# A rebuilt start of the program in a fused attention and expert kernel: loads in order of need, statistics a batch at a time, splits on VectorE, keys loaded before queries

## The chip, the core and the metric

The kernel runs on one core of a Trainium2 chip. The core has a matrix engine (TensorE, PE in the profile; its weight loads are PEld), VectorE (DVE), ScalarE (ACT), GpSimd (POOL) and SyncE (SP), which here only issues DMAs. The metric is the time of one execution on the device in microseconds, the median of several. Each engine works through its own list in program order; a semaphore makes an instruction, and all behind it on that engine, wait for another engine or a DMA.

## The reference

For 4 batches of 1,024 rows of 128 floats the reference computes

```
mod = silu(c) @ wmod -> sa, ca, ga, sb, cb, gb per batch   (ga, gb kept at least 0.25 in size)
h   = layernorm(x) * (1 + ca) + sa
Q, K, V = h @ W.T + b, 16 heads of 8
scores  = Q K^T / sqrt(8) + lambda * (tanh(Q) J) tanh(K)^T, causal, softmax
x   = x + ga * (attended @ Wo.T + bo)
h   = layernorm(x) * (1 + cb) + sb
expert = argmax(h @ centroids.T), one of 8;  y = layernorm(h) through that expert's two layers of 512
x   = x + gb * (alpha * y + (1 - alpha) * h)
```

## The kernel before, in words

Names: `X` holds all rows. `T32` holds Q, K, tanh(K), tanh(Q)J (and tanh(Q)) of one batch as 128 channels by 1,024 rows; `T16` holds each of the four as a sum of three bf16 parts. A score is a bf16 product over 96 rows of parts; the parts go to DRAM (`q_parts`, `k_parts`) and come back into `stacks`, one region for each of the four groups of four heads, query side and key side apart (`load_group`: 3 loads for queries, 6 for keys, one for values `Vs`). A softmax without overflow needs each query's maximum first: for every group a list of 22 "maxima" chunks (`CHUNKS`, kind m) is multiplied on PE and reduced on VectorE (L1443, L1450), the result is split in three bf16 parts (`mparts`, L1462 to L1464), turned on PE (kind T), copied to `mrow` and sent by four DMAs (L376) into `stacks` as 3 more rows, against three rows of ones on the key side (99 rows in all). Then PE makes scores (L1014), ScalarE the exponentials (L785), PE the products with the values (L989).

The program has a start ("prologue"), then 4 bodies of 4 groups ("first", two "middle" in a loop, "last"), then the experts' tiles. In a body, the maxima of the group after are woven into the attention of the present one, by a planner (`schedule`): it is given a cost for each item (`D_COST`, `P_COST`, `R_COST`) and spreads the items so that VectorE's costs grow in step with PE's. Items: P (projections of the next batch, in group 0), D (VectorE alone) and R (after attention). `schedule(prep, post, last)` puts the items of `POST_AT` or `POST_LAST` in the groups.

The prologue, which is what changes. SP loads the first batch of X, wmod, the four weights, the other batches, and then `JB`, a 128x128 block diagonal matrix, by 16 small loads into a zeroed tile (L359). ScalarE issues 7 loads of `rows` (vectors that PE turns into columns, `cols`), 4 of biases (`bias_in`, the last of them `b2_b`, 512 KB), and, after its first activation, the expert weights W1 and W2 and beta. VectorE: `base` (L1146), `cols` (L1149), silu of the conditioning (L1153 on), weights out of PSUM (L1158), statistics of batch 0 (L1164, then 15 steps of a Newton root, `moment_step`, each waiting for the one before), `JL` (L1172), `modT`, normed rows (L1140), and the evacuation of the ten P items in the order X, Q, K, V, J. After the small product for `modT` (L862) PE makes the wide one (L865) that gives the other modulations, `MB`, before the projections. GpSimd splits the first of the four tensors (L574 to L579), VectorE the other three (`split0`, three steps each: subtract, cast, subtract), then come `conditioning` (which turns the wide product into `MB`) and the statistics of the three other batches (L1164 again, 24 at once). SP stores each tensor's parts when it is split, waits for GpSimd to say that all are stored, and loads groups 0 and 1 (L366, L369). PE turns the expert weights (`turn_weights`, 16 in all, evacuated by ScalarE, L762 and L764): four before the maxima of group 0, one after each of the first twelve chunks. GpSimd writes the rows of ones (L563), two regions at the start, two after `fold_beta` (L590 to L598: beta through W1, and b1), and adds `ga_bo` to X (`residual`, L611).

## Time and profile before

| | us |
|---|---|
| median of 3 runs | 845.47 (844.82 to 854.59) |
| the profiled execution, its own time | 847.08 |
| its span, first to last instruction | 845.2 |
| first projection on PE | 27.09 |
| first chunk of maxima on PE | 67.38 |
| first score of the first attention group | 106.38 |

| engine | busy us | share |
|---|---|---|
| PE | 694.1 | 82% |
| DVE | 620.3 | 73% |
| ACT | 455.9 | 54% |
| POOL | 250.6 | 30% |

A timeline row gives start, length, engine, line and operation, what is written and read, and in brackets the idle time before it with what ended it. A shared name covers several tiles (arenaA, arenaB), and a helper's line (L1111 is every `tensor_tensor`) covers many operations, so one goes by time and shape.

### The profile page before, as it was taken

To read this page: it belongs to the slowest core of one execution; us is meant where nothing else is said; L and a number is where in the kernel's file an instruction comes from. 1 tells how busy PE (TensorE), PEld (TensorE's weight loads), DVE (VectorE), ACT (ScalarE), POOL (GpSimd) and SP (SyncE) were. 2 spreads that over 40 slices of the span, in tenths; PEclk is the share of its full clock that TensorE was granted. 3 is DMA by queue.
4 is the path that set the end of the run, shared out by engine and by line. 5 is a ranking of instruction groups with operands and counts; after the bars stand their busy time and mean duration, and the time that the engine had idled before them with its cause. 6 is when DMAs were issued, how large, how long until landed. Compare 5 with 4: busy or idle time off the path is not lost.

```text
span 845.2 us, 17049 instructions
## 1 busy us (share of the span) xinstructions
PE 694.1 (82%) x5087; PEld 348.3 (41%) x5087; DVE 620.3 (73%) x1485; ACT 455.9 (54%) x1077; POOL 250.6 (30%) x210
## 2 busy tenths in 40 slices
PE   3517597999999899888798987999988879886694
PEld 1314143333343334233333333433423326876694
DVE  6698977778778887878487878778887812786453
ACT  0213065667665575546456754557564668644482
POOL 5205803930000860114028502030001400453643
PEclk9758589999999999989799999999999979997898
DMA  9389190419533237525403392436302243621520
GB/s 260 132 209 255 43 177 1 124 55 168 113 69 61 77 104 145 97 53 134 102 14 92 90 183 57 86 109 144 123 16 90 113 147 105 194 65 66 191 77 12
DMA packets 51305, 91.96 MB, mean 109 GB/s; under 512 B 9005, under 2 KB 24945, under 8 KB 50700
## 3 DMA queue, kind: packets, MB, share of 16 engines
q1 hardware_dynamic: 41904, 67.56, 34.2%
q0 software_dynamic: 6400, 17.86, 6.8%
q10 hardware_dynamic: 2908, 5.41, 2.0%
q8 instruction: 46, 0.75, 0.4%
q14 instruction: 47, 0.39, 0.2%
HBM read 51.05 MB, written 37.90 MB: 105 GB/s over the span
## 4 chain that ended last, share of the span: by engine, by line
PE 51%; DVE 22%; issue 11%; DMA 6%; SPq 5%; ACT 2%; DVEq 1%; POOL 0%; ACTq 0%; POOLq 0%
PE PS L989 13%; PE PS L1014 12%; PE PS L952 10%; DVE PS L1443 5%; PE PS L1065 4%; PE PS L1076 3%; DVE arenaB L1111 3%; SPq L376 3%; DVE block_max L1450 2%; PE PS L1018 2%; DMA arenaA<-mrow 2%; ACT arenaA L785 2%; PE PS L892 2%; DMA arenaB<-r_den 1%; DVE arenaA L1111 1%
## 5 line engine op out<-in xcount | busy, mean ns | idle before, releaser
L785 ACT ACTIVATE arenaA<-PS 128x512 f32<-128x512 f32 (+3 forms) x768 | 332.0, 494 | 251.4 <-PE PS L1018 190.4
L1443 DVE CUSTOM_DVE_ANT_0 PS<-PS,mask 128x1024 f32<-128x1024 f32 (+3 forms) x256 | 261.3, 1037 | 71.9 <-PE PS L952 63.9
L1014 PE MATMUL PS<-arenaA 99*128 99x512 bf16 (+3 forms) x768 | 225.4, 340 | 17.3 <-DMA arenaA<-mrow 7.9
L952 PE MATMUL PS<-arenaA 96*128 96x512 bf16 (+3 forms) x768 | 202.7, 341 | 36.3 <-DVE maxima L1443 19.8
L989 PE MATMUL PS<-arenaA,Vs 128*9 128x512 f32 (+3 forms) x1536 | 164.2, 504 | 0.0
L1014 PEld LDWEIGHTS PS<-arenaA 99*128 99x128 bf16 x768 | 73.8, 99 | 207.3 <-ACT arenaA L785 122.5
L1450 DVE TENSOR_REDUCE block_max<-PS 128x8 f32<-128x1024 f32 (+1 forms) x96 | 100.3, 1045 | 24.3 <-PE PS L957 23.1
L952 PEld LDWEIGHTS PS<-arenaA 96*128 96x128 bf16 x768 | 66.5, 101 | 107.3 <-DVE maxima L1443 46.5
L1018 PE MATMUL PS<-after,identb 128*128 128x128 bf16 x512 | 107.6, 227 | 0.0
L574 POOL TENSOR_TENSOR arenaB<-arenaB 128x1024 f32<-128x1024 f32 x13 | 27.9, 2144 | 197.6 <-ACT arenaB L724 197.5
L677 POOL DMA_INDIRECT out_dram<-arenaA x46 | 46.1, 1001 | 98.2 <-DVE arenaA L1111 94.8
L831 ACT ACTIVATE arenaA<-PS,b1p 128x128 f32<-128x128 f32 x184 | 52.9, 372 | 38.0 <-PE PS L1065 37.8
L1065 PE MATMUL PS<-arenaA 128*128 128x128 f32 x368 | 53.3, 292 | 15.0 <-DVE arenaA L1532 14.9
L630 POOL TENSOR_TENSOR arenaB<-arenaB,MB 128x1024 f32<-128x1024 f32 x4 | 9.5, 2366 | 159.7 <-DVE arenaB L1111 159.7
L1065 PEld LDWEIGHTS PS<-arenaA 128*128 128x128 f32 x368 | 47.9, 204 | 18.2 <-DVE arenaA L1532 18.2
L1018 PEld LDWEIGHTS PS<-after,identb 128*128 128x128 bf16 x512 | 52.0, 101 | 4.0 <-issue 0.2
L1076 PE MATMUL PS<-arenaA 128*128 x368 | 51.7, 287 | 1.8 <-issue 1.8
L957 PE MATMUL PS<-identb,after 128*128 128x128 bf16 x256 | 51.5, 230 | 0.0
L1076 PEld LDWEIGHTS PS<-arenaA 128*128 128x128 f32 x368 | 47.8, 203 | 2.4 <-issue 2.4
L989 PEld LDWEIGHTS PS<-arenaA,Vs 128*9 128x9 f32 x1536 | 23.7, 89 | 51.2 <-ACT arenaA L785 24.8
L654 POOL DMA_INDIRECT by_expert<-arenaB,slot x32 | 31.2, 977 | 29.3 <-issue 14.3
L1532 DVE COPY arenaA<-PS 128x128 f32<-128x128 f32 x46 | 13.0, 285 | 32.7 <-PE PS L1056 32.0
(179 smaller groups left out, 726.7 us busy)
## 6 DMA issues: line engine op xcount, KB each, us to landing
arenaA<-k_parts SPq DMA_DIRECT2D x96, 128.0 KB, 7.3
arenaA<-by_expert SPq DMA_DIRECT2D x46, 192.5 KB, 3.4
o_raw<-OT SPq DMA_DIRECT2D x32, 256.0 KB, 2.2
arenaA<-q_parts SPq DMA_DIRECT2D x16, 384.0 KB, 5.1
q_parts<-arenaB POOLq DMA_DIRECT2D x18, 256.0 KB, 3.8
k_parts<-arenaB POOLq DMA_DIRECT2D x18, 256.0 KB, 3.8
arenaA<-q_parts SPq DMA_DIRECT2D x16, 256.0 KB, 5.7
w_turned<-arenaA SPq DMA_DIRECT2D x2, 2048.0 KB, 9.4
```

The lines of the kernel that those rows point to most:

```text
L677: g.indirect_dma_start(out_rows, bass.IndirectOffsetOnAxis(ap=XSI[n % NX][:, 3 * D:3 * D + 1], axis=0), YS[:, n % U, :], None, bounds_chec ...
L785: a.activation(PT[:, u % EB, h, off:HALF], PS[:, 4 + n % SB_, off:HALF], ACT.Exp).then_inc(exp_ok, 1)
L831: last = a.activation(HR[:, n % 3, k * P:(k + 1) * P], PS[:, 3 + n % 2, k * P:(k + 1) * P], ACT.Relu, bias=b1p[:, bass.ds(expert[n] * FC + ...
L952: last = mm(PS[:, place + c0 // HALF, at:at + c1 - c0], SQ(g, h)[0:KROWS, t * P:(t + 1) * P], SK(g, h)[0:KROWS, c0:c1], start=(at == 0), s ...
L957: last = mm(diag, after[:, :], identb[:, :], start=False, stop=True, skip_group_check=True)
L989: last = mm(PS[32 * h:32 * h + VW, 7, off:HALF], Vs[:, g, (kb * HG + h) * VW:(kb * HG + h + 1) * VW], PT[:, u % EB, h, off:HALF], start=(k ...
L1014: last = mm(bank[:, off:HALF], SK(g, h)[0:MROWS, kb * P:(kb + 1) * P], SQ(g, h)[0:MROWS, qc * HALF + off:(qc + 1) * HALF], start=True, sto ...
L1018: last = mm(bank[:, off:off + P], identb[:, :], after[:, :], start=False, stop=True, skip_group_check=True)
L1065: last = mm(PS[:, 3 + n % 2, k * P:(k + 1) * P], W1C[n % 3][:, k * P:(k + 1) * P], XT[:, n % 3, :], start=(k == 0), stop=True, skip_group_ ...
L1076: last = mm(PS[:, 6 + n % 2, 0:D], HR[:, n % 3, k * P:(k + 1) * P], W2T[:, bass.ds(expert[n] * FF + k * P, P)], start=(k == 0), stop=(k == ...
L1443: v.tensor_tensor_reduce(out=src, in0=src, in1=mask[:, S - n:S], scale=1.0, scalar=-3e38, op0=ALU.add, op1=ALU.max, accum_out=maxima[:, pl ...
L1450: v.tensor_reduce(block_max[:, place % 2, heads[0]:heads[-1] + 1, t, 0:t + 1], src.rearrange("p h (c q) -> p h c q", q=P), AX.X, ALU.max). ...
```

## The change

1. SP loads the weights ahead of wmod, `J` in one load (`Jr`, 128x8) behind them, then the other batches; rows of ones come by DMA from `onesb` (two regions early, two just before groups 2 and 3 are loaded), and W1 and W2 now come on SP's queue. W1 is read so that each partition gets 4 adjacent rows (2 KB runs). ScalarE issues 5 loads of rows, the same 4 of biases, then `b1c` (b1 in runs of 4 floats) and beta, all ahead of its first activation.
2. VectorE begins with the statistics of batch 0; `JL` is made from `Jr` and a mask `of_head`; the weights' evacuation is ScalarE's; only the small product for `modT` stands ahead of the projections, the wide one behind them.
3. P items in the order X, Q, K, J, V. Statistics of batch 1 lie between them, those of batches 2 and 3 in groups 1 and 2 of the first body.
4. All four splits of batch 0 on VectorE, with ScalarE casting the middle part of two. Key parts are waited for and loaded apart from and ahead of query parts for group 0.
5. Six weights are turned ahead of the maxima; `fold_beta` works in pieces of a quarter or a half; no ones on GpSimd.

What moves on VectorE at the start of the program. Before (`silu` is the conditioning, `lnt` the root of the statistics, `arenaB<-silu` the wide copy of silu for the wide product):

```order
L1146 TENSOR_SCALAR base<-iota_f 128x8 [waits consts_ok]
L1149 COPY cols<-PS 128x62 [waits cols_ps]
L1151 TENSOR_SCALAR bqs<-cols 128x1 [waits cols_ok]
L1153 TENSOR_SCALAR silu<-silu 128x4 [waits silu_e]
L1154 RECIPROCAL silu<-silu 128x4 [waits dve_chain]
L1111 TENSOR_TENSOR silu<-silu,cols 128x4 [waits dve_chain]
L1156 COPY arenaB<-silu 128x512 [waits dve_chain]
L1158 COPY wT<-PS 128x512 [waits wT_ps]
L1164 BN_STATS stat<-X 128x6 [waits x_in0]
```

The same place now, from the first statistics on (L1137 is the helper's line now):

```order
L1174 BN_STATS stat<-X 128x6 [waits x_in0]
...
L1185 COPY cols<-PS 128x22 [waits cols_ps,dve_chain]
...
L1189 TENSOR_SCALAR bqs<-cols 128x1 [waits cols_ok,dve_chain]
L1191 TENSOR_SCALAR silu<-silu 128x4 [waits silu_e]
L1192 RECIPROCAL silu<-silu 128x4 [waits dve_chain]
L1137 TENSOR_TENSOR silu<-silu,cols 128x4 [waits dve_chain]
L1166 TENSOR_SCALAR arenaB<-X,lnt 128x128 x8
L1495 COPY arenaA<-silu 128x512 [waits silu3_ok]
L1499 SCALAR_TENSOR_TENSOR JL<-Jr,lam_c,of_head 128x128 [waits bias_in,consts_ok,j_in]
L1502 COPY modT<-PS 128x4 [waits mod_ps]
L1503 TENSOR_SCALAR modT<-PS 128x4
L1233 TENSOR_SCALAR HT<-PS,modT 128x512 [waits max_ps,modT_ok]
```

Statistics and root (not all rows shown) went ahead of the conditioning, `base` and `wT` left this stretch, and JL waits for the bias loads with the normed rows already made.

VectorE's splits now, after the second K evacuation (L1241 are the two J evacuations, the last L1137 a V evacuation):

```order
L1239 TENSOR_SCALAR arenaB<-PS,cols 128x512 [waits max_ps,dve_chain]
L1137 TENSOR_TENSOR arenaB<-arenaB 128x1024 [waits max_used,first_ok]
L1516 CAST arenaB<-arenaB 128x1024 [waits r1_ok]
L1137 TENSOR_TENSOR arenaB<-arenaB 128x1024 [waits split0_step,r1_ok]
L1137 TENSOR_TENSOR arenaB<-arenaB 128x1024 [waits first_ok]
L1241 COPY arenaB<-PS 128x512 [waits max_ps] x2
L1516 CAST arenaB<-arenaB 128x1024 [waits max_used,r1_ok]
L1137 TENSOR_TENSOR arenaB<-arenaB 128x1024 [waits split0_step,r1_ok]
L1137 TENSOR_TENSOR arenaB<-arenaB 128x1024 [waits first_ok] x2
L1137 TENSOR_TENSOR arenaB<-arenaB 128x1024 [waits mid_ok,r1_ok] x2
L1137 TENSOR_TENSOR arenaB<-PS,bv_b 128x16x8 [waits max_ps]
```

Before, V and J were evacuated first, then three splits of subtract, cast, subtract followed.

SP between the last stored parts and the loads of group 0, now:

```order
L412 DMA q_parts<-arenaB 16x8x1024 [waits split0_ok]
L412 DMA q_parts<-arenaB 16x8x1024 x2
L376 DMA arenaA<-k_parts 16x4x1024 [waits parts0_k]
L376 DMA arenaA<-k_parts 16x4x1024 x5
L376 DMA arenaA<-q_parts 48x4x1024 [waits parts0_q]
L376 DMA arenaA<-q_parts 32x4x1024
L386 DMA Vs<-arenaB 128x288 [waits va_ok]
```

Before, the 3 query loads came first and all ten waited for all twelve stores.

The diff, cut to what the text speaks of:

```
@@ tiles
+        Jr = sb("Jr", [P, HD])
+        of_head = sb("of_head", [P, H])
+        b1c = sb("b1c", [P, E, FC])
@@ planner
-        FIRST = [("P", 0, k) for k in range(len(PREP))] + [("m", 0, k) for k in range(NM)] + \
+        FIRST = [("P", 0, PREP.index(step)) for step in ("X0", "X1", "Q0", "Q1", "K0", "K1", "J0", "J1", "V0", "V1")] + [("m", 0, k) for k in range(NM)] + \
+        STATS_AT = {g: ((4, "D", ("stats_b", b_)),) + tuple((5 + n // 2, "D", ("root_b", b_, n)) for n in range(MOMENTS)) for g, b_ in ((1, 2), (2, 3))}
+        D_COST = {("stats_b", b_): 1600 for b_ in (2, 3)} | dict(denominators=870, ...
-        BODIES = dict(first=schedule(True, False, False), middle=schedule(True, True, False), last=schedule(False, True, True))
+        BODIES = dict(first=schedule(True, STATS_AT, False), middle=schedule(True, POST_AT, False), last=schedule(False, POST_LAST, True))
@@ SyncE
-            sp.dma_start(wm[:, :], wmod).then_inc(w_in, 16)
             for n, w in enumerate((Wq, Wk, Wv, Wo)):
                 sp.dma_start(wraw[:, n, :], w).then_inc(w_in, 16)
+            sp.dma_start(wm[:, :], wmod).then_inc(w_in, 16)
+            sp.dma_start(Jr[:, :], J.rearrange("h r c -> (h r) c")).then_inc(j_in, 16)
...
-            for h in range(H):
-                sp.dma_start(JB[h * HD:(h + 1) * HD, h * HD:(h + 1) * HD], J[h]).then_inc(j_in, 16)
+            def ones(r):
+                sp.dma_start(stacks[KROWS:MROWS, r, 1, :, :], onesb[0:(MROWS - KROWS) * 32, :]).then_inc(first_ones if r < 2 else ones_ok, 16)
+            sp.wait_ge(consts_ok, 1)
+            ones(0)
+            ones(1)
+            sp.dma_start(W1r.rearrange("p (e c) d -> p e (c d)", e=E), W1.rearrange("e (p c) d -> p e (c d)", c=FC)).then_inc(w1_in, 16)
+            sp.dma_start(Aap[:, 20480:24576].rearrange("p (e f) -> p e f", e=E), W2.rearrange("e d n -> d e n")).then_inc(w2_in, 16)
...
-            prepared(0)
-            for g in range(2):
-                load_group(0, g)
+            sp.wait_ge(parts0_k, PARTS_OUT // 2)
+            load_side(0, 0, 1)
+            sp.wait_ge(parts0_q, PARTS_OUT // 2)
+            load_side(0, 0, 0)
+            sp.wait_ge(va_ok, 1)
+            load_values(0)
+            load_group(0, 1)
...
             for g in range(2, NG):
+                ones(g)
                 load_group(0, g)
@@ GpSimd
-            def ones(r):
-                if r:
-                    pool.wait_ge(ones_ok, r)
-                g.memset(stacks[KROWS:MROWS, r, 1, :, :], 1.0).then_inc(ones_ok, 1)
-            ones(0)
-            ones(1)
-            split(0, 0, split0_q)
...
-            ones(2)
-            ones(3)
+            pool.wait_ge(b1_ok, 1)
             residual(0)
@@ ScalarE
+            act.dma_start(b1c[:, :, :], b1.rearrange("e (p c) -> p e c", c=FC)).then_inc(b1_in, 16)
+            act.dma_start(OT[:, :, :].rearrange("p a q -> p (a q)"), row(beta.rearrange("e d -> (e d)")).to_broadcast([P, E * D])).then_inc(beta_in, 16)
             act.wait_ge(cols_ok, 1)
...
+            act.wait_ge(wT_ps, 1)
+            a.activation(wT[:, :, :].rearrange("p n d -> p (n d)"), PS[:, 1, :], ACT.Copy).then_inc(wT_ok, 1)
...
+            for n in (2, 3):
+                k = TENSORS[n][0]
+                act.wait_ge(r1_ok, n + 1)
+                a.activation(T16[:, k, 1, :], T32[:, k, :], ACT.Copy).then_inc(mid_ok, 1)
@@ VectorE
+            first_item(0)
+            first_item(1)
+            batch_stats(1)
+            for n in range(MOMENTS):
+                if n % 5 == 0:
+                    first_item(2 + n // 5)
+                batch_root(1, n)
+            first_item(5)
+            rest0(0)
+            middle0(0)
+            last0(0)
+            rest0(1)
...
+            first_item(8)
+            first_item(9)
+            conditioning()
```

## Rows read from the trace of the kernel before

**Rows 1.** Timeline (columns as told above), the first projections and first chunk of maxima on PE.
```profile
27.09 6.67 PE L892 MATMUL PS<-HT,wT 128*128 128x512 f32 x8 [0.96 <-DVEq L1428]
67.38 0.69 PE L952 MATMUL PS<-arenaA 96*128 96x512 bf16 x2 [5.69 <-DMA Vs<-arenaB]
106.38 0.58 PE L1014 MATMUL PS<-arenaA 99*128 99x512 bf16 x1 [1.33 <-DMA arenaA<-mrow]
```
**Rows 2.** Timeline, VectorE, from the start to the normed rows' evacuation.
```profile
5.76 3.56 DVE L1146 TENSOR_SCALAR base<-iota_f 128x8 f32<-128x8 f32 x1 [4.45 <-POOL identb L556]
...
14.26 1.64 DVE L1164 BATCH_NORM_STATS2 stat<-X 128x6 f32<-128x128 f32 x8
...
19.00 0.17 DVE L1136 SCALAR_TENSOR_TENSOR lnt<-lnt 128x8 f32<-128x8 f32 x1
21.43 0.29 DVE L1172 TENSOR_SCALAR JL<-JB,lam_c 128x128 f32<-128x128 f32 x1 [2.27 <-DMA JB<-in_L_attn_J_attn_dram]
...
21.90 2.14 DVE L1140 TENSOR_SCALAR arenaB<-X,lnt 128x128 f32<-128x128 f32 x8
25.31 1.66 DVE L1214 TENSOR_SCALAR HT<-PS,modT 128x512 f32<-128x512 f32 x2 [1.27 <-PE PS L879]
```
**Rows 3.** DMA issues at 0.9 and 5.1 us: size, and us from issue to landing.
```profile
X<-in_L_attn_x_dram SPq DMA_DIRECT2D x1, 512.0 KB, 4.5
...
b_b<-in_L_ffn_b_dram ACTq DMA_DIRECT2D x1, 512.0 KB, 9.4
```
**Rows 4.** Timeline, GpSimd.
```profile
5.78 7.07 POOL L563 MEMSET arenaA<- 3x4096 bf16 x2
38.09 2.12 POOL L579 TENSOR_TENSOR arenaB<-arenaB 128x1024 bf16<-128x1024 f32 x1
73.18 8.87 POOL L590 TENSOR_TENSOR arenaA<-arenaA,OT 128x4096 f32<-128x4096 f32 x1 [32.97 <-ACT arenaA L762]
...
92.79 7.07 POOL L563 MEMSET arenaA<- 3x4096 bf16 x2
100.16 2.34 POOL L611 TENSOR_TENSOR X<-X,ga_bo 128x1024 f32<-128x1024 f32 x1 [0.30 <-POOL arenaA L563]
```
**Rows 5.** Timeline, VectorE, evacuation of Q, splits, conditioning.
```profile
29.20 0.75 DVE L1218 TENSOR_SCALAR arenaB<-PS,bqs 128x512 f32<-128x512 f32 x1 [2.22 <-PE PS L892]
...
36.61 1.38 DVE L1222 COPY arenaB<-PS 128x512 f32<-128x512 f32 x2
38.14 3.16 DVE L1111 TENSOR_TENSOR arenaB<-arenaB 128x1024 f32<-128x1024 f32 x1
...
45.18 2.36 DVE L1111 TENSOR_TENSOR arenaB<-arenaB 128x1024 bf16<-128x1024 f32 x2
...
48.30 1.22 DVE L1111 TENSOR_TENSOR arenaB<-arenaB 128x1024 bf16<-128x1024 f32 x1
```
**Rows 6.** Timeline, SyncE's queue: first loads of group 0.
```profile
54.09 1.30 SPq L366 DMA_DIRECT2D arenaA<-q_parts  x3
```
**Rows 7.** Timeline, VectorE: the split of a group's maxima, group 0 and a later group.
```profile
92.73 3.61 DVE L1462 TENSOR_SCALAR mparts<-maxima 128x32 bf16<-128x32 f32 x1
...
100.10 0.83 DVE L1443 CUSTOM_DVE_ANT_0 PS<-PS,mask 128x640 f32<-128x640 f32 x1
...
208.48 0.18 DVE L1462 TENSOR_SCALAR mparts<-maxima 128x32 bf16<-128x32 f32 x1
...
209.30 0.83 DVE L1443 CUSTOM_DVE_ANT_0 PS<-PS,mask 128x640 f32<-128x640 f32 x1
```
**Rows 8.** Windows: us, busy us of PE, PEld, DVE, ACT, POOL, PEclk, DMA share, GB/s.
```profile
181.50:211.80 30.30, 29.71 (x245) 11.96 (x243) 23.93 (x45) 21.57 (x51) 0.00 (x0) 1.00 0.69 122
242.20:286.40 44.20, 40.72 (x285) 16.70 (x281) 35.99 (x70) 26.40 (x57) 10.80 (x8) 1.00 0.34 72
317.10:361.00 43.90, 36.94 (x282) 15.39 (x281) 37.04 (x94) 23.19 (x56) 4.46 (x2) 0.96 0.60 116
399.00:451.30 52.30, 44.24 (x285) 18.00 (x277) 36.25 (x71) 26.41 (x55) 10.90 (x8) 0.90 0.27 63
```

More of the change, by code:

```diff
@@ L589, in fold_beta @@
                 beta_b = OT[:, :, :].rearrange("p a q -> p (a q)").rearrange("p (e o d) -> p e o d", e=E, o=1).to_broadcast([P, E, FC, D])
[L590 to L591 removed]
+                done, chunks, half = 0, 4, D // 2
+                for k in range(4):
+                    g.tensor_tensor(w1[:, 2 * k:2 * k + 2], w1[:, 2 * k:2 * k + 2], beta_b[:, 2 * k:2 * k + 2], ALU.mult).then_inc(b1_step, 1)
                 while half:
[L594 to L604 removed]
+                    done += chunks
+                    pool.wait_ge(b1_step, done)
+                    chunks = 2 if half == D // 2 else 1
+                    for k in range(chunks):
+                        part = slice(k * E * FC // chunks, (k + 1) * E * FC // chunks)
+                        g.tensor_tensor(W1r[:, part, 0:half], W1r[:, part, 0:half], W1r[:, part, half:2 * half], ALU.add).then_inc(b1_step, 1)
+                    half //= 2
+                pool.wait_ge(b1_step, done + chunks)
+                g.tensor_tensor(b1p[:, :], W1r[:, :, 0], b1c[:, :, :].rearrange("p e c -> p (e c)"), ALU.add).then_inc(b1_ok, 1)
+            fold_beta()
             def residual(b):
@@ L761, in _ @@
                 if k < E:
[L762 removed]
+                    a.activation(dst, src, ACT.Identity, scale=gamma_c[:, k:k + 1]).then_inc(w_ev, 1)
                 else:
@@ L913, in after_attention @@
                     for t in range(TB):
-                        last = mm(PS[:, bank, t * E:(t + 1) * E], AT[:, t * P:(t + 1) * P], cols[:, 48:56], start=(t == 0),
+                        last = mm(PS[:, bank, t * E:(t + 1) * E], AT[:, t * P:(t + 1) * P], cent_c, start=(t == 0),
                                   stop=True, skip_group_check=True)
@@ L1144, in _, with batch_stats, batch_root @@
             v.memset(block_max[:, :, :, :, :], -3e38)
-            dve.wait_ge(consts_ok, 1)
-            v.tensor_scalar(base[:, :], iota_e, float(PHASES[0][2]), None, ALU.mult)
+            def batch_stats(b):
+                dve.wait_ge(x_in[b], 16)
+                for t in range(TB):
+                    last = v.bn_stats(stat[:, b * TB + t, :], X[:, b * TB + t, :])
+                last.then_inc(bn_ok, 1)
+            def batch_root(b, n):
+                if n == 0:
+                    dve.wait_ge(bn_ok, b + 1)
+                link(moment_step(n, lambda k: lnt[:, k, b * TB:(b + 1) * TB], stat[:, b * TB:(b + 1) * TB, :]))
+            batch_stats(0)
+            for n in range(7):
+                batch_root(0, n)
             dve.wait_ge(cols_ps, 1)
-            v.tensor_copy(cols[:, 0:62], PS[:, 0, 0:62]).then_inc(cols_ok, 1)
+            v.tensor_copy(cols[:, :], PS[:, 0, 0:22]).then_inc(cols_ok, 1)
+            for n in range(7, MOMENTS):
+                batch_root(0, n)
             dve.wait_ge(cols_ok, 1)
-            v.tensor_scalar(bqs[:, :], cols[:, 60:61], HD ** -0.5, None, ALU.mult)
+            v.tensor_scalar(bqs[:, :], bq_c, HD ** -0.5, None, ALU.mult)
             dve.wait_ge(silu_e, 1)
@@ L1219, in projected @@
                 elif what == "K":
-                    v.tensor_scalar(T32[:, 1, part], src, cols[:, 61:62], None, ALU.add).then_inc(max_used, 1)
+                    v.tensor_scalar(T32[:, 1, part], src, bk_c, None, ALU.add).then_inc(max_used, 1)
                 elif what == "J":
@@ L1473, in split0, with rest0 @@
+            dve.wait_ge(mod_ps, 1)
+            v.tensor_copy(modT[:, 0, :], PS[:, 2, 0:B])
+            v.tensor_scalar(modT[:, 1, :], PS[:, 2, B:2 * B], 1.0, None, ALU.add).then_inc(modT_ok, 1)
+            dve.wait_ge(modT_ok, 1)
+            def rest0(n):
                 k = TENSORS[n][0]
                 dve.wait_ge(first_ok, n + 1)
-                a = T32[:, k, :]
-                steps = 2 * (n - 1)
-                tt(a, a, T16[:, k, 0, :], ALU.subtract).then_inc(split0_step, 1)
-                dve.wait_ge(split0_step, steps + 1)
@@ L1479, in split0 @@
-                v.tensor_copy(T16[:, k, 1, :], a).then_inc(split0_step, 1)
-                dve.wait_ge(split0_step, steps + 2)
-                tt(T16[:, k, 2, :], a, T16[:, k, 1, :], ALU.subtract).then_inc(split0_ok, 1)
-            for i, (kind, ahead, k) in enumerate(FIRST):
-                maximum(kind, ahead, k, i, FIRST_BANKS[i][0], ahead)
-                if i == len(PREP) - 1:
-                    for n in range(1, 4):
-                        split0(n)
-                    conditioning()
-                    statistics(1, B, 2)
+                tt(T32[:, k, :], T32[:, k, :], T16[:, k, 0, :], ALU.subtract).then_inc(r1_ok, 1)
@@ L1491, in attention @@
+            first_item(7)
+            middle0(1)
+            last0(1)
+            rest0(2)
+            rest0(3)
+            last0(2)
+            last0(3)
+            first_item(8)
+            first_item(9)
+            conditioning()
+            for i in range(len(PREP), len(FIRST)):
+                first_item(i)
             def attention(b, body):
```

169 lines of the change are left out of this document (87 added, 82 removed).

## The prediction, made before the changed kernel ran

> **What bounds the kernel now.** I read the stages by time first: the chain of waits and the timeline say that nothing before the first score can overlap the attention, since PE must have the maxima of group 0 first. So a microsecond off the prologue is one off the kernel, unless a later group gives it back. Three marks divide the prologue [rows 1]: the first projection at 27.09 us, the first chunk of maxima at 67.38 (PE had waited for a load, `Vs<-arenaB`), the first score at 106.38. Then VectorE's timeline, since it makes what each mark waits for. Up to 27.09 the reader is to see [rows 2]: `base`, 8 numbers a partition, takes 3.56 us, while GpSimd writes ones for 7.07 us from 5.78 on [rows 4]; a small step of the silu is held likewise. The statistics begin at 14.26 although X had landed at 0.95 + 4.5 = 5.45 [rows 3], and `JL` waits 2.27 for the 16 small J loads. From 27 to 50 VectorE evacuates and splits [rows 5]; the first load of parts is issued at 54.09 [rows 6], 13.3 us ahead of the chunk at 67.38. At 92.73 the maxima are done, and their split lasts till 100.10, 7.37 us, where a later group takes 208.48 to 209.30, 0.82 [rows 7]: GpSimd wrote ones from 92.79 for 7.07 us [rows 4].
>
> **Part 1, up to the first projection.** VectorE after the change, added up. Start 5.45, X landed. Eight statistics and the root: 14.26 to 19.17 (19.00 + 0.17) before, 4.91, unchanged in count [rows 2]: to 10.4. `cols` in their middle: no row shows it undisturbed; it lies between 0.15, like the small copies near it, and the 1.48 that it took from 7.84 during the ones; I take 0.2, since GpSimd has then nothing but its constants. bqs and three silu steps, 0.2 each: 11.4. The activation that they need waits behind two more DMA issues on ScalarE (b1c, beta), about 0.6 each, against two fewer row loads, 0.3 each: some 8.5 us, covered by the root, which ends at 10.6. Normed rows 2.14: 13.6. The wide copy of silu, 0.43: 14.0. Now `JL` waits for all bias loads. The last, b2_b, landed at 5.16 + 9.4 = 14.56 [rows 3] and is issued about 0.6 earlier: 14.0. JL 0.29 and two copies for modT 0.3: 14.7. The two evacuations of turned rows 1.66 [rows 2] and handing on: 16.5. With the old landing of 14.56 it would be 17.1; I take 17.0, near that, because SP's queue moves as many bytes beside it as before. The first projection moves from 27.09 to 17.0, **minus 10.1** (9 to 10.7). The wide product, 6 us of PE, lay in VectorE's shadow before; behind V it still has conditioning's turn on VectorE to wait for, so nothing.
>
> **Part 2, to the key parts stored.** From 16.9 VectorE has no free time that counts: statistics and root of batch 1, 4.9; four evacuations of Q and K at 0.75, 3.0; J 1.38; splits. A whole split is 45.18 to 48.30, 3.1, its two subtractions 2.36 [rows 5]. Two whole and two without the cast: 6.2 + 4.8 = 11.0. Sum 20.3, with waits on semaphores 20.9: the last split ends at 37.8, before at 48.30 + 1.22 = 49.52. PE has the fourth projection done 6.7 us after its start, at 23.7, and VectorE comes to it at 24.6; ScalarE's casts of 1.05 lie beside the subtractions. That is 1.6 more off. The gain contains 1.9 for the first subtraction of before, which took 3.16 and not 1.22 beside GpSimd's from 38.09 on [rows 4, 5], and pays for batch 1's statistics. The keys are ready one subtraction earlier than the queries, at 36.6. From the last split to the first load were 54.09 - 49.52 = 4.6 us (stores issued, landed); the same puts the first key load at 41.2, **minus 12.9** in all. Loading keys and values moves no bytes: the ten loads of group 0 took 13.3 us from the first issue, and PE needs all ten. I keep 13.3 and add 0.2, as the last query stores (landed by about 42.8) stand in front of the keys on SP's queue; bounds 0 and 1.6. First chunk at 54.7. Conditioning and V, some 10 us, end at 48 under that load; if the load were 6 us shorter, they would be next. Six weights turned instead of four are under it too. The statistics that stood here before (24 at once and a root, 8.1 us, VectorE) were hidden by the same load: taking them out gives nothing, and they now cost elsewhere (part 4).
>
> **Part 3, the maxima of group 0.** 67.38 to 92.73 is 25.4 us, VectorE full; the reductions read PSUM and were not longer beside GpSimd. The same: 80.1. The split of the maxima then: 0.82 if undisturbed, 7.37 if as before. GpSimd's `fold_beta` began at 73.18, 5.8 after the first chunk; with six weights ahead the eighth is evacuated two chunks sooner, 3.9 after, 58.6. It ran till 92.79, 19.6 us; in pieces the same elements, so 78.2, and `residual` 2.34 [rows 4] till 80.5. So one operation may be held, by 0.4, at worst by one whole instruction of 2.34, or of some 2.2 (a quarter of the 8.87) if fold_beta comes late. I take 2.0, nearer to the undisturbed row: **minus 5.4** (-6.5 to -3). First score at 106.38 - 12.7 - 5.4 = 88.3.
>
> **Part 4, what the groups give back.** Groups 1 and 2 of the first body each get 8 statistics and a root, 4.9 us of VectorE (4.5 busy). Such a group takes 30.3 us with PE busy 29.71 and VectorE 23.93 [rows 8], so 28.4 busy still fits: lower bound nothing. Upper bound: the group from 317.1 to 361.0 has 13.1 more on VectorE (and 7.2 more on PE) and takes 13.6 more, 1.04 per us: 4.7 each. The planner books 1600 + 15 x 110 = 3.25 us of the 4.9; the other 1.65 come unplanned where PE has few free banks. I take 1.0 of it a group, nearer to the plain group, in which VectorE waits for PE: **plus 2.0** (0 to 9.4). The rows of ones by DMA and the GpSimd memsets after group 0's maxima cost nothing later: GpSimd is idle for tens of us there.
>
> **Sum.** -12.7 - 5.4 + 2.0 = -16.1 on the profiled execution's 847.08: 831.0. That execution is 1.6 above the median of the runs, so 829.4, say **829**, 1.9% less.
>
> **Rivals.**
> - *The statistics are free.* PE bounds the groups, and the maxima's split is undisturbed: part 4 nothing, part 3 -6.5. 847.08 - 19.2 - 1.6 = 826, 825 with the lower end of part 1. For it: 6.4 us of VectorE idle in a plain group. Against: 4.9 us in one piece of 8 steps.
> - *VectorE bounds groups 1 and 2.* At the 84% of the group from 317.1 on (37.04 of 43.90), 28.4 busy need 33.8 us, 3.5 more each: 834; at the upper bound 837.
> - *The start does not move as it says.* `JL` stands ahead of `modT` and waits for b2_b, on a queue that now competes with everything SP issues, and W1 and W2 (4 MB) stand ahead of the parts on SP's own queue. If b2_b lands at 20 rather than 14, or the first stores wait as long: 835 to 840. Against: DMA was as full before, until 30 us. b1c's runs of 16 bytes stand behind b2_b, and their reader is GpSimd at 58.
> - *Slower: PE falls to its half clock in the first body.* The granted clock was 1.00 (2.4 GHz) in 181.5 to 211.8 and 0.90 in 399.0 to 451.3, where a group 0 took 52.3 us against 44.2 for the same work at 1.00 from 242.2 on [rows 8]: 8 us by the clock. If VectorE's statistics let PE pause enough in groups 1 and 2, its 29.7 us of work would take twice that at 1.2 GHz. It decides from 16 us lost, a little over half a group at 1.2 GHz; both groups would make it 872. Against: the busier group from 317.1 kept 0.96. The Trainium skill, "TensorE: Matmul & The Clock Gate", section "HAM oscillation — how this bites in real kernels", describes such gaps that return each turn; no gap here is a load's.
>
> **Chances.** A difference of 2% (16.9 us, below 828.6) is about what a measurement of this kernel tells from none. Forecast, 826.5 to 832.5: 0.47, of which 0.24 under 828.6, as its middle lies just above. Statistics free: 0.20. VectorE bounds: 0.20. The start held: 0.09. Clock: 0.04. Faster by over 2%: 0.24 + 0.20 = 0.44; within 2%: 0.23 + 0.20 + 0.09 = 0.52; slower 0.04. The range, 822 to 838, takes in parts 1 to 3 at their lower ends and the vector-bound case, and leaves out most of the held start and the clock.
>
> **What would show it.** In the new profile: first statistics at 5.5 and first projection at 17 (later, with `JL<-` waiting for a DMA: the third rival); last subtraction at 38; first key load at 41; first chunk at 54.7; the `mparts` operations under 1 us each but one; first score at 88; maxima sent 30.3 us apart before and about 31.3 in groups 1 and 2 now. I am wrong if the first chunk comes under 51 or over 58, if the two groups grow by over 3 us each, or if from group 3 on the spacing differs.

## The result and the profile after

The changed kernel took 848.28 us (median of 20 runs, 844.01 to 852.68) against 844.2 of the kernel before on the same chip (20 runs, 838.55 to 854.59): ratio 1.0056, 95% interval 1.0034 to 1.0077. Forecast were 829 us and a range of 822 to 838. The start became shorter as forecast (its first send of maxima came 18.2 us earlier), and two groups of the attention gave 15.4 us back.

| | before | after |
|---|---|---|
| profiled execution, its span | 847.08, 845.2 | 846.77, 845.0 |
| first projection | 27.09 | 16.14 |
| first chunk of maxima | 67.38 | 54.45 |
| maxima of group 0 sent (SP's issue to `stacks`) | 101.69 | 83.53 |
| first score | 106.38 | 88.11 |
| from that send to the next ones: groups 0, 1, 2, 3 | 49.1, 30.7, 30.3, 30.4 | 49.1, 42.5, 33.9, 30.4 |

The issue of the four DMAs that send a group's maxima (`arenaA<-mrow`) comes once a group; I use the distance between two of them as the length of a group.

The start first. The timeline of PE in the changed kernel has the marks that answer to [rows 1]:
```profile
10.05 1.12 PE L877 MATMUL PS<-ident,arenaA 128*128 128x128 f32 x4 [3.80 <-DMA arenaA<-in_L_wmod_dram]
16.14 5.72 PE L915 MATMUL PS<-HT,wT 128*128 128x512 f32 x8 [1.05 <-DVEq L1451]
54.45 0.69 PE L975 MATMUL PS<-arenaA 96*128 96x512 bf16 x2 [8.98 <-DMA Vs<-arenaB]
88.11 0.59 PE L1040 MATMUL PS<-arenaA 99*128 99x512 bf16 x1 [1.22 <-DMA arenaA<-mrow]
```
VectorE's timeline, the rows that answer to [rows 2] and [rows 5]: statistics from X's landing on, `JL` with no wait before it, the five subtractions in one row, and `base`, 0.17 us where it was 3.56:
```profile
5.28 1.65 DVE L1174 BATCH_NORM_STATS2 stat<-X 128x6 f32<-128x128 f32 x8 [3.98 <-DMA X<-in_L_attn_x_dram]
13.26 0.34 DVE L1499 SCALAR_TENSOR_TENSOR JL<-Jr,lam_c,of_head 128x128 f32<-128x128 f32 x1
14.35 1.59 DVE L1233 TENSOR_SCALAR HT<-PS,modT 128x512 f32<-128x512 f32 x2 [0.61 <-PE PS L900]
31.17 5.92 DVE L1137 TENSOR_TENSOR arenaB<-arenaB 128x1024 bf16<-128x1024 f32 x5
41.14 0.17 DVE L1200 TENSOR_SCALAR base<-iota_f 128x8 f32<-128x8 f32 x1
```
SyncE's first loads, which answer to [rows 6]: keys at 40.29 and not 54.09.
```profile
40.29 3.34 SPq L376 DMA_DIRECT2D arenaA<-k_parts  x6
43.67 1.39 SPq L376 DMA_DIRECT2D arenaA<-q_parts  x3
45.10 0.55 SPq L386 DMA_DIRECT2D Vs<-arenaB  x1
```
And the split of the maxima, which answers to [rows 7], first on VectorE, then what GpSimd did then:
```profile
80.98 0.32 DVE L1485 TENSOR_SCALAR mparts<-maxima 128x32 bf16<-128x32 f32 x1
...
81.94 0.83 DVE L1466 CUSTOM_DVE_ANT_0 PS<-PS,mask 128x640 f32<-128x640 f32 x1
```
```profile
58.61 9.33 POOL L606 TENSOR_TENSOR arenaA<-arenaA,OT 128x1024 f32<-128x1024 f32 x4 [52.71 <-ACT arenaA L781]
68.02 10.39 POOL L614 TENSOR_TENSOR arenaA<-arenaA 128x1024 f32<-128x1024 f32 x8
78.92 2.34 POOL L625 TENSOR_TENSOR X<-X,ga_bo 128x1024 f32<-128x1024 f32 x1 [0.17 <-POOL b1p L617]
```
The split takes 0.96 us (80.98 to 81.94), and only its first step is longer than the 0.18 of [rows 7]: it ends at 81.30, when `residual` ends (78.92 + 2.34 = 81.26).

Then the groups. Windows of the changed kernel from one send to the next, groups 1, 2 and 3 (columns as in [rows 8]), then two pieces of group 1:
```profile
132.50:175.00 42.50, 34.66 (x245) 12.45 (x241) 35.80 (x71) 23.86 (x53) 23.67 (x19) 0.87 0.25 75
175.00:208.90 33.90, 30.72 (x245) 12.03 (x241) 27.54 (x71) 21.52 (x50) 0.00 (x0) 1.00 0.68 119
208.90:239.30 30.40, 29.57 (x245) 11.89 (x241) 24.03 (x46) 21.02 (x49) 0.00 (x0) 1.00 0.36 76
152.00:157.00 5.00, 3.72 (x22) 1.51 (x21) 4.53 (x9) 2.19 (x4) 4.39 (x5) 0.64 0.24 62
157.00:162.00 5.00, 2.86 (x10) 0.41 (x11) 4.72 (x7) 1.68 (x3) 1.46 (x1) 0.50 0.50 151
```
Group 1 of before, the same view, which is not among the rows ahead of the prediction:
```profile
150.80:181.50 30.70, 29.08 (x241) 11.93 (x241) 23.94 (x45) 22.59 (x51) 24.18 (x19) 1.00 0.36 108
```
The reader is to see two things. Both groups got the same 26 operations of VectorE (71 for 45), but group 2's busy time grew by 3.6 us and group 1's by 11.9. And in group 1 GpSimd is busy for 24 us in either kernel, in group 2 not at all. VectorE's timeline in group 1 shows where the 8.3 us are:
```profile
143.42 2.01 DVE L1147 TENSOR_SCALAR lnt<-lnt 128x8 f32<-128x8 f32 x1
...
147.14 2.62 DVE L1155 TENSOR_SCALAR lnt<-lnt 128x8 int32<-128x8 int32 x1
...
151.14 0.60 DVE L1159 SCALAR_TENSOR_TENSOR lnt<-lnt 128x8 f32<-128x8 f32 x1
...
153.04 0.91 DVE L1162 SCALAR_TENSOR_TENSOR lnt<-lnt 128x8 f32<-128x8 f32 x1
...
155.79 2.71 DVE L1159 SCALAR_TENSOR_TENSOR lnt<-lnt 128x8 f32<-128x8 f32 x1
```
Each of these is a root step on 8 numbers a partition. In group 2, where GpSimd does nothing, the second of them takes 0.17 us:
```profile
187.48 0.17 DVE L1155 TENSOR_SCALAR lnt<-lnt 128x8 int32<-128x8 int32 x1
```
In group 1 GpSimd meanwhile splits batch 1's tensors (L587, L590, L592):
```profile
143.27 2.13 POOL L592 TENSOR_TENSOR arenaB<-arenaB 128x1024 bf16<-128x1024 f32 x1
...
147.59 2.14 POOL L587 TENSOR_TENSOR arenaB<-arenaB 128x1024 f32<-128x1024 f32 x1
149.80 1.91 POOL L590 TENSOR_TENSOR arenaB<-arenaB,zero 128x1024 bf16<-128x1024 f32 x1
151.79 2.14 POOL L592 TENSOR_TENSOR arenaB<-arenaB 128x1024 bf16<-128x1024 f32 x1
...
156.11 2.35 POOL L625 TENSOR_TENSOR X<-X,ga_bo 128x1024 f32<-128x1024 f32 x1
```
143.42 + 2.01 = 145.43 and 143.27 + 2.13 = 145.40; 147.14 + 2.62 = 149.76 and 147.59 + 2.14 = 149.73; 155.79 + 2.71 = 158.50 and 156.11 + 2.35 = 158.46. Each long step ends with a GpSimd operation. The five, less 0.17 each, make 8.0 us, and the three operations of the first step (0.61 together at 142.77, 0.33 in group 2) another 0.3. The eight statistics, all beside GpSimd's work in group 1 and beside none in group 2, did not get longer:
```profile
139.96 1.64 DVE L1174 BATCH_NORM_STATS2 stat<-X 128x6 f32<-128x128 f32 x8
...
182.43 1.64 DVE L1174 BATCH_NORM_STATS2 stat<-X 128x6 f32<-128x128 f32 x8
```
What PE waited for in group 2 of the changed kernel, which has no such hold (columns: us in total, times, longest; the same view of before has one wait for VectorE there, 0.4 us):
```profile
PE PS L975 <- DVE maxima L1466: 1.5, 4, 0.5
PE PS L975 <- DVE block_max L1473: 1.1, 2, 0.7
```

### The profile page after: what moved, and what is told of

Same layout as the page of the kernel before. It is cut to its first block, busy times and chain, and to the rows that moved or that the text cites. A ratio compares the mean times of both kernels' runs of the same rounds, so it can differ in the third digit from the quotient of the medians.

```text
span 845.0 us, 17085 instructions
## 1 busy us (share of the span) xinstructions
PE 702.9 (83%) x5087; PEld 349.8 (41%) x5087; DVE 618.9 (73%) x1521; ACT 457.9 (54%) x1079; POOL 230.8 (27%) x209
## 4 chain that ended last, share of the span: by engine, by line
PE 51%; DVE 26%; issue 10%; DMA 5%; SPq 3%; ACT 2%; DVEq 1%; POOL 0%; ACTq 0%; POOLq 0%
PE PS L1014 13%; PE PS L1040 12%; PE PS L975 11%; DVE PS L1466 6%; PE PS L1091 4%; PE PS L1102 3%; DVE block_max L1473 3%; DVE arenaB L1137 3%; PE PS L1044 2%; SPq L393 2%; ACT arenaA L804 2%; DVE arenaA L1137 1%; DMA arenaB<-r_den 1%; DMA arenaA<-mrow 1%; PE PS L980 1%
## 5 line engine op out<-in xcount | busy, mean ns | idle before, releaser
L1466 DVE CUSTOM_DVE_ANT_0 PS<-PS,mask 128x1024 f32<-128x1024 f32 (+3 forms) x256 | 261.4, 1036 | 76.2 <-PE PS L975 68.0
L975 PE MATMUL PS<-arenaA 96*128 96x512 bf16 (+3 forms) x768 | 206.6, 347 | 46.0 <-DVE maxima L1466 20.4
L1040 PE MATMUL PS<-arenaA 99*128 99x512 bf16 (+3 forms) x768 | 228.1, 344 | 17.7 <-DMA arenaA<-mrow 7.4
L1014 PE MATMUL PS<-arenaA,Vs 128*9 128x512 f32 (+3 forms) x1536 | 166.2, 510 | 0.0
L1473 DVE TENSOR_REDUCE block_max<-PS 128x8 f32<-128x1024 f32 (+1 forms) x96 | 100.3, 1045 | 23.7 <-PE PS L980 22.4
L587 POOL TENSOR_TENSOR arenaB<-arenaB 128x1024 f32<-128x1024 f32 x12 | 25.7, 2142 | 194.7 <-ACT arenaB L739 194.6
L1598 DVE COPY arenaA<-PS 128x128 f32<-128x128 f32 x46 | 13.0, 284 | 34.9 <-PE PS L1082 34.4
```

What stands on the lines that cost most here:

```text
L975: last = mm(PS[:, place + c0 // HALF, at:at + c1 - c0], SQ(g, h)[0:KROWS, t * P:(t + 1) * P], SK(g, h)[0:KROWS, c0:c1], start=(at == 0), s ...
L1014: last = mm(PS[32 * h:32 * h + VW, 7, off:HALF], Vs[:, g, (kb * HG + h) * VW:(kb * HG + h + 1) * VW], PT[:, u % EB, h, off:HALF], start=(k ...
L1040: last = mm(bank[:, off:HALF], SK(g, h)[0:MROWS, kb * P:(kb + 1) * P], SQ(g, h)[0:MROWS, qc * HALF + off:(qc + 1) * HALF], start=True, sto ...
L1466: v.tensor_tensor_reduce(out=src, in0=src, in1=mask[:, S - n:S], scale=1.0, scalar=-3e38, op0=ALU.add, op1=ALU.max, accum_out=maxima[:, pl ...
L1473: v.tensor_reduce(block_max[:, place % 2, heads[0]:heads[-1] + 1, t, 0:t + 1], src.rearrange("p h (c q) -> p h c q", q=P), AX.X, ALU.max). ...
```

## The experiments

All kernels were compared with the kernel before on their own chip; there it took 863.3 us (runs 1 to 4), 843.6 (5 to 8), 863.8 (9, 10) and 862.7 (11, 12), so across these sets ratios are compared and not times. Distances between sends are from the profiled executions.

**1. All statistics in the prologue** (from the changed kernel; one root for batches 2 and 3 behind the conditioning). The code is shortened, here and in the next.
```
-BODIES = dict(first=schedule(True, STATS_AT, False), ...
+BODIES = dict(first=schedule(True, {}, False), ...
 conditioning()
+batch_stats(2); batch_stats(3)
+for n in range(MOMENTS): link(moment_step(n, <both batches>))
```

> The changed kernel, but the statistics of batches 2 and 3 stand in the prologue, 16 at once and one root, after the conditioning (VectorE was idle there from 47.3 to 55.3 us in the changed kernel), and none in groups 1 and 2. Theory L (the gain of 18 us at the first score is lost in groups 1 and 2, where the root's small steps are held by GpSimd and the maxima behind them come late): first chunk of maxima still at 54.4, maxima sent at about 83.5, 132.6, 163.3, 193.7, so groups 1 and 2 take 30.7 and 30.4 us; median 0.981 to 0.985 of the kernel before, some 830 us. Theory C (the gain is given back by something later in the program, whatever stands in groups 1 and 2): the two groups are short, but the end stays at 844 to 848.

Measured: 847.94 us, ratio 0.9819 (0.9776 to 0.9862). Maxima sent at 83.64, groups 1 and 2 30.32 and 30.33. The window of group 1, with GpSimd as busy as ever:
```profile
132.80:163.10 30.30, 29.14 (x241) 11.92 (x241) 23.93 (x45) 22.56 (x51) 24.00 (x19) 1.00 0.36 108
```
The start keeps its gain with the statistics in it (they lie under the load of group 0, 47.29 on), and what groups 1 and 2 had lost goes with the statistics. The splits alone cost group 1 nothing: 30.3 us, as in a group without them.

**2. Statistics in groups 2 and 3**, where GpSimd is idle.
```
-... for g, b_ in ((1, 2), (2, 3))}
+... for g, b_ in ((2, 2), (3, 3))}
```

> The changed kernel, with the statistics of batches 2 and 3 in groups 2 and 3 of the first body instead of 1 and 2: the same instructions, but GpSimd, whose splits of batch 1 end at about 158 us, is then idle. Theory L (GpSimd's hold on the shared port is what made group 1 take 42.5 us): group 1 falls to 30.7, group 2 stays at 33.9, group 3 rises from 30.4 to about 34; sum -8, some 840 us. Theory B (VectorE has too much work in such a group, wherever it is): group 1 30.7, and the two others share some 15 us, as groups 1 and 2 do now; the time stays at 848. No root step over 0.3 us under L in any group.

Measured: 858.4, ratio 0.9941 (0.9908 to 0.9974). Groups 1, 2, 3: 30.36, 33.92, 33.97, as the theory of the hold expected. The same work costs 3.6 in a group without GpSimd and 11.8 in one with it.

**3. The same with the whole cost booked** in the planner: `root_b` at 215 ns and more instead of 110, statistics 1650 instead of 1600.

> As the run before it (statistics in groups 2 and 3), but the planner is told what the steps take: 1650 ns for the eight statistics, 215 for a root step (400 and 310 for the first two) in place of 1600 and 110, so that the maxima's chunks are placed later behind them. If the 3.5 us that group 2 lost in the changed kernel come from the 1.65 us that were not planned: groups 2 and 3 fall to about 31.5 each, -4 to -5 us against that run. If they come from the work itself: 33.5 to 34 each, and no difference in the time.

Measured: 855.99, ratio 0.9909 (0.9878 to 0.9941). Groups 2 and 3: 33.77 and 33.82. The unbooked 1.65 us was not the cause of the 3.6.

**4. Before, with only the rows of ones by DMA** (the memsets of `ones` on GpSimd replaced by the changed kernel's four loads from `onesb`).

> The kernel before with one part of the change alone: the rows of ones come by DMA, not by GpSimd. Where GpSimd's memsets held VectorE: the split of the first maxima takes 0.8 to 1.2 us and not 7.37, the first operation on base and the silu step under 0.3 us and not 3.56 and 3.28. The first gives 6.4 us to the end. The second gives nothing if JL, which waits for the 16 small J loads till 21.4, is what bounds the first projection (27.1 as before); if VectorE's own work bounds it, the first projection comes at some 21 and the end 6 us sooner still. So 838 (0.992) or 832 (0.985).

Measured: 863.77, ratio 0.9997 (0.9968 to 1.0026), far from the expected gain. `base` and the silu step took 0.17 us and the statistics began at 10.31 rather than 14.26, but VectorE's timeline then shows
```profile
25.56 0.29 DVE L1165 TENSOR_SCALAR JL<-JB,lam_c 128x128 f32<-128x128 f32 x1 [10.35 <-DMA JB<-in_L_attn_J_attn_dram]
```
against 21.43 in [rows 2]. So the front was bound by the 16 loads of J, and the memsets' hold was hidden behind them. The maxima's split took 2.9 us (its last step ended with `residual`), and they were sent at 99.53, 2.2 earlier than in the first trace of before and 1.1 later than in the second (experiment 11). So the missing memsets alone start no projection earlier; the statistics' place, the memsets and the one load of J had to go together, and part 1 of the prediction priced only the first two.

**5. The changed kernel with GpSimd's splits of batch 1 cut to one column** (leaves that part of the computation out; DMAs stay).
```
-a = T32[:, k, :]
+N = 1 if isinstance(b, int) and b == 1 else S
+a = T32[:, k, 0:N]
... (and 0:N in the three operations)
```

> The changed kernel, statistics in groups 1 and 2 as there, but GpSimd's three operations on each tensor of batch 1 work on one column in place of 1,024 (so the parts of batch 1 beyond the first are not made, and the output is not the reference's). Nothing on VectorE, PE or in the planner's order differs. Theory L (port held by GpSimd): no root step over 0.3 us in group 1, group 1 takes 33.9 us as group 2 does, and not 42.5, and the PE clock stays at 1.00 in it; 8 to 9 us less than the changed kernel. Theory P (it is the place: group 1 has other things late, as the o_raw store that waited 14 us or the loads of groups 2 and 3): group 1 stays above 38.

Measured: 839.3, ratio 0.996 (0.993 to 0.9991). No root step took over 0.17 us. Group 1 took 38.6 us, 3.9 less than in the changed kernel and not the expected 33.9; its granted clock was 0.96 and not 1.00. By its length alone the other theory (over 38) would be right. The rows give a reason of another kind: the stores of all parts came in a bunch at 124 to 135, and the maxima's DMA, issued at 128.34, stood among them:
```profile
135.75 0.61 PE L1041 MATMUL PS<-arenaA 99*128 99x512 bf16 x1 [3.69 <-DMA arenaA<-mrow]
```
```profile
132.00:136.00 4.00, 0.31 (x5) 0.13 (x2) 0.56 (x1) 0.00 (x0) 3.23 (x8) 0.95 0.86 240
```
38.56 less PE's 3.69 of waiting is 34.9, a microsecond over group 2's 33.9. So the hold is gone with GpSimd's work, as the theory says, but what the hold cost can't be read from this run, since the edit moved the stores too. Group 0 also became shorter, 44.7 in place of 49.1: the splits of batch 1 begin in it, and in the changed kernel two steps of the split of group 1's maxima were held there:
```profile
121.77 2.01 DVE L1486 SCALAR_TENSOR_TENSOR mres<-maxima,mparts 128x32 f32<-128x32 f32 x1
123.81 0.18 DVE L1487 CAST mparts<-mres 128x32 bf16<-128x32 f32 x1
124.03 1.76 DVE L1137 TENSOR_TENSOR mparts<-mres,mparts 128x32 bf16<-128x32 f32 x1
```
With the cut they took 0.19 each. The kernel before has the same hold in its group 0 (2.01 and 1.76 us), so it is no part of what the change lost.

**6. The statistics one tile and one root step at a time**, in groups 2 and 3, from item 2 on (before: 8 at item 4, then two steps an item).

> As the run with statistics in groups 2 and 3, but spread: eight items of one statistic each, one planner step apart, and one root step at a time where two stood together, over 23 of 33 steps and not 12. If the 3.5 us a group come from clumps (a chunk of maxima waits behind 1.64 us or two linked steps, and PE has no free bank): 31 to 32 us in groups 2 and 3. If they come from the sum of VectorE's work: 33.5 to 34. Worse than 34 if each piece between two chunks costs its own wait (0.21 us stood between a root step and the chunk behind it).

Measured: 836.86, ratio 0.9911 (0.9881 to 0.9941). Groups 2 and 3: 33.21 and 33.31. Spreading saves 0.7 us of 3.6 a group; the rest stays in both orders that were tried.

**7. Root steps alone in groups 1 and 2**, the 16 statistics in the prologue.

> The changed kernel with the eight statistics of batches 2 and 3 in the prologue (3.3 us of VectorE's idle time under the load), and only the 15 root steps in groups 1 and 2. Theory L: the root's steps are what GpSimd holds, so group 1 keeps most of its loss, 38 to 41 us; group 2, with 3.2 us in place of 4.9, takes 32 to 33. If it were the block of 1.64 us that puts PE off: groups 1 and 2 near 31.

Measured: 844.17, ratio 1.0 (0.9984 to 1.0016). Group 1: 43.7, above the expected 38 to 41; group 2: 33.1. The chain of small steps is enough for all of group 1's loss (six of them took 0.68 to 2.91 us), VectorE and then GpSimd:
```profile
147.98 2.54 DVE L1159 SCALAR_TENSOR_TENSOR lnt<-lnt 128x8 f32<-128x8 f32 x1
...
152.74 1.98 DVE L1137 TENSOR_TENSOR lnt<-lnt 128x8 f32<-128x8 f32 x1
...
156.35 2.91 DVE L1137 TENSOR_TENSOR lnt<-lnt 128x8 f32<-128x8 f32 x1
```
```profile
148.34 2.14 POOL L587 TENSOR_TENSOR arenaB<-arenaB 128x1024 f32<-128x1024 f32 x1
150.56 1.92 POOL L590 TENSOR_TENSOR arenaB<-arenaB,zero 128x1024 bf16<-128x1024 f32 x1
152.56 2.14 POOL L592 TENSOR_TENSOR arenaB<-arenaB 128x1024 bf16<-128x1024 f32 x1
155.29 1.57 POOL L633 DMA_DIRECT2D q_parts<-arenaB  x3 [0.59 <-POOL arenaB L592]
156.87 2.36 POOL L625 TENSOR_TENSOR X<-X,ga_bo 128x1024 f32<-128x1024 f32 x1
```
The three end at 150.52, 154.72 and 159.26, and GpSimd's operations at 150.48, 154.70 and 159.23. The first and the last began 0.36 and 0.52 us before the GpSimd operation with which they end, while GpSimd was still issuing DMAs: a step can be held for longer than that operation lasts. Whether the issuing of DMAs holds it too is not shown.
Windows of the same stretch:
```profile
148.00:152.00 4.00, 1.86 (x13) 0.44 (x13) 3.75 (x6) 1.84 (x4) 3.91 (x3) 1.00 0.63 185
152.00:156.00 4.00, 1.85 (x9) 1.03 (x9) 3.68 (x5) 0.60 (x1) 3.33 (x4) 0.51 0.00 0
```
PE was busy 1.86 of 4 us at a granted clock of 1.00 (2.4 GHz), and then the clock fell to 0.5 (1.2 GHz).

**8. Queries before keys**: group 0 loaded as before the change, after all stores.
```
 sp.wait_ge(parts0_k, PARTS_OUT // 2)
-load_side(0, 0, 1)
 sp.wait_ge(parts0_q, PARTS_OUT // 2)
-load_side(0, 0, 0)
 sp.wait_ge(va_ok, 1)
-load_values(0)
+load_group(0, 0)
```

> The changed kernel with one part undone: all twelve stores are waited for, then queries, keys, values are loaded, as before. The wait for the last query part costs: keys were issued at 40.3 us with the last query store issued till 39.8 and landed by some 42.5. So first load at 42.7 (+2.4) and first chunk of maxima at 56 to 57 in place of 54.4, if what the load takes (14.2 us from the first issue in the changed kernel) does not depend on order; 54.4 again if the wait is made good by the load.

Measured: 851.75, ratio 1.009 (1.0063 to 1.0118). First load at 43.18, first chunk at 56.61, maxima sent at 85.64: loading keys first is worth 2.2 us of part 2's gain, near the 2.4 expected.

**9 and 10. The changed kernel and experiment 1 on one chip.**

> The changed kernel with nothing altered, beside the next one on one chip. Theory (a root step that meets a GpSimd operation waits for its end): the maxima are sent again some 42.5 us apart over group 1 and 33.9 us over group 2, and the time stands at 1.000 to 1.008 of the kernel before. A rival, that the loss of group 1 belongs to one chip's clock and not to the program, expects group 1 near 31 to 34 us here and a ratio under 0.995.

> The version with all statistics in the prologue, a second time, beside the unchanged changed kernel on one chip. Theory: groups 1 and 2 take 30.3 us each, 15.7 us less together than in the changed kernel, and the time is 0.979 to 0.988 of the kernel before, so 14 to 20 us under the changed kernel's on this chip. The rival, that the later groups give part of it back when the start is earlier, expects 5 to 10 us under it and a ratio near 0.992.

Measured: 867.81, ratio 1.0056 (1.0035 to 1.0077), groups 1 and 2 43.3 and 33.9; and 850.55, ratio 0.9836 (0.9801 to 0.9871), groups 30.3 and 30.3. The loss came again on another chip, so it belongs to the program, the lowered clock in group 1 (0.84 over the group) with it. From the first send to the fifth the two differ by 156.78 - 139.91 = 16.9 us, and the medians by 17.3.

**11 and 12. The kernel before and experiment 1 on one chip**, since the marks promised more than the medians gave.

> The kernel before, unaltered, for a second trace of it on the chip of the next run. In the runs so far the marks add up to more gain than the times show: 18.3 us in the start and 0.4 in groups 1 and 2 for the version with all statistics in the prologue, but 14 to 16 us in the medians. Theory S (scatter: the first trace of before was a slow execution, 3 us over its median, and its tail of 169.8 us a short one): the time from the fifth send of the maxima to the last, and the tail after the last, agree here within 2 us with those of the next run. Theory G (the changed start gives 2 to 5 us back later, in the bodies or in the experts' part): the tail is again near 169.8 us here against 172 in the next run, or the groups from 3 on are shorter here by over 2 us. The ratio to itself is 1.000 either way.

> The version with all statistics in the prologue once more, beside a trace of the kernel before from the same chip. Theory S expects from the fifth send of the maxima on the same as before within 2 us, and a ratio near 1 - 18.7/844 = 0.978. Theory G expects 2 to 5 us more there than before, and a ratio of 0.981 to 0.985.

Measured: 863.13, ratio 1.0021 (0.9987 to 1.0054); 849.26, ratio 0.983 (0.9789 to 0.987). The ratio is the one of theory G, but the larger part of the missing gain is one that neither theory named. The second trace of the kernel before sent its first maxima at 98.44, not 101.69. Its split of the maxima, VectorE then GpSimd:
```profile
92.97 0.18 DVE L1462 TENSOR_SCALAR mparts<-maxima 128x32 bf16<-128x32 f32 x1
93.19 0.19 DVE L1463 SCALAR_TENSOR_TENSOR mres<-maxima,mparts 128x32 f32<-128x32 f32 x1
93.42 3.23 DVE L1464 CAST mparts<-mres 128x32 bf16<-128x32 f32 x1
```
```profile
93.10 7.07 POOL L563 MEMSET arenaA<- 3x4096 bf16 x2
```
The first step began 0.13 us ahead of the memset and took 0.18; in [rows 7] and [rows 4] it began 0.06 ahead and took 3.61. So here one memset held one conversion, and there each of the two memsets held one. So the start gains 18.2 us against the one trace and some 15 against the other. From the fifth send to the last the two kernels agree (450.2 and 450.6), as theory S said; the tail behind the last send is 2.3 longer (171.3 and 173.6; 169.8 and 172.1 in the first pair), as theory G said. Over all traces the two sets overlap, though: 169.8 to 171.5 without the changed start (before twice, experiment 4) and 170.8 to 173.6 with it (the eleven others). A longer tail of about 1 us is likely, 2.3 is not shown, and its cause is open.

## Why the prediction was wrong

- **Part 1, right.** First projection 16.14, forecast 17.0 (9 to 10.7 earlier; it was 10.95). VectorE came to `JL` at 13.26 and did not wait, so the third rival did not occur. The term "now `JL` waits for all bias loads" did not bind: b2_b was issued at 4.20 and landed 7.5 us later, at 11.7 and not 14.0, and VectorE itself came 0.7 earlier than my sum.
- **Part 2, right.** Last subtraction at 37.1 (forecast 37.8), key load 40.29 (41.2), first chunk 54.45 (54.7). Load and chunk are 14.2 apart, forecast 13.5: 0.7 against me, inside the bounds. Experiment 8 confirms the order of loads, experiment 1 that taking the statistics out from under the load gains nothing.
- **Part 3, right in the trace, wrong as a base.** The split fell from 7.37 to 0.96 us, of which 1.2 went to a longer run of chunks (54.45 to 80.98 is 26.5, before 25.4; why is not known), so the send moved by 18.2 and 18.1 was forecast. But 7.37 was one execution's value: 3.87 in the other trace (92.97 to 96.84). I took the hold of each conversion for fixed and the profiled execution for a typical one but for 1.6 us. The start of one operation against a memset, 0.06 or 0.13 us apart, goes with a difference of 3.3 us in the send. By the second trace the start gains about 15. The section of the Trainium skill that the prediction names, "Who interferes with whom", says that the order of issue decides who blocks. The traces do not show that by their recorded starts: VectorE's step began first in both, and was held in one.
- **Part 4, the step that failed:** "The planner books 1600 + 15 x 110 = 3.25 us of the 4.9 ... I take 1.0 of it a group ... plus 2.0 (0 to 9.4)". Measured: 11.8 in group 1 and 3.6 in group 2. The size of the work was read from rows of the prologue where GpSimd was idle, and the group was read from group 2 and a later one. GpSimd in group 1 did not enter the sum, though the trace that I predicted from shows it busy there for 24.2 of 30.7 us. In part 3 the hold was read from rows, and the rule of the Trainium skill, "SBUF — State Buffer", section "Who interferes with whom", stood beside it: a tensor_scalar in a two-port mode, or an instruction of two SBUF inputs against a GpSimd reader, waits for the whole of the other instruction if that was issued first. The trace of group 1 agrees in that every long step, of each of these forms, ends with a GpSimd operation; two of them (147.14 and 155.79) began 0.45 and 0.32 us before it. I did not ask the question of the steps that the change adds. Asked there, the rows give the size: each unheld step is soon followed by another, so nearly every GpSimd operation meets one. The five between 143.27 and 158.46 last 10.7 us together, and operations of the same lengths ran in group 1 of before. That is an estimate made afterwards. The runs show it: 8.3 held in group 1 (the trace), none with GpSimd idle (experiment 2), none with its work cut (5), and 10.1 with the root steps alone (7).
- **Group 2**, 3.6, is the rival "VectorE bounds groups 1 and 2" (3.5 a group), to which I gave 0.20. Its number is right, and my reason for a small price, that only unbooked work costs, is refuted by experiment 3. A group with VectorE at 24 us busy has no free 4 us: PE was busy 29.71 of 30.30, and what VectorE gets besides delays its reductions, on which PE's next chunk waits: PE waited 2.6 us for them in group 2 (0.4 before). VectorE was busy 27.54 of 33.90, 81%, against the rival's 84%. The other 1.4 of the 3.6 is in part PE's own busy time, 30.72 against 29.71; no run takes it apart.
- **The clock rival** came in a small form: the granted clock fell to 0.50 for some 10 us of group 1 after PE had waited for VectorE. It adds little: what group 2 lost plus what was held in group 1 makes what group 1 lost against 30.7, in each of three traces: 3.6 + 8.3 = 11.9 and 11.8 in the changed kernel, 3.6 + 8.8 = 12.4 and 12.6 in experiment 9, 2.8 + 10.1 = 12.9 and 13.0 in experiment 7. The rival's 872 was wrong by its own numbers: twice 29.7 for 30.3, in two groups, on 827.4 makes 886.
- **The sum.** Between the forecast, 829, and the median, 848.3, lie 19.3 us, and part 4 is 13.4 of them (15.4 less the 2.0 that I put). Most of the rest is the base: the profiled execution stood 2.9 above the median of 20 runs and not 1.6, and its 7.37 us split was not typical. From trace to trace, -18.2 or -14.9 in the start (101.69 or 98.44 to 83.53), +11.8, +3.6 and the first pair's tail of +2.3 give -0.5 or +2.8. The profiled executions differ by -0.3, the medians by +4.1 (2.9 to 6.5). What is left of the 4.1 is not accounted for.

The best version is experiment 1: the change with all statistics left in the prologue, 1.6 to 1.8% faster than before in three comparisons. Its first send came at 83.3 to 84.3 us in three traces, so it keeps what parts 1 to 3 gain, and its groups are as long as before.
